# Graph attention and mixture-of-experts layer: row gathers without fills, slot sums by three strided reductions, partial step fourth

## The reference

```python
feat = einsum('ni,rhid->rnhd', layernorm(x), conv_weights)      # 8 types, 4 heads, 64 each
e = leaky_relu(el[type, src] + er[type, dst], 0.2)              # one score per edge and head
alpha = exp(e - segment_max(e, dst)) / segment_sum(exp(...), dst)
x = x + segment_sum(alpha * feat[type, src], dst) + h_bias
xf = layernorm(x)
cw = the two largest of softmax(xf @ gate_w + gate_b), else 0   # [3750, 8]
x = x + sum over e of cw[:, e] * (gelu(xf @ W1[e] + b1[e]) @ W2[e] + b2[e])
```

## Time and profile before

| | |
|---|---|
| median of 3 runs | 1844.96 us |
| profiled execution: its time, its span | 1841.54 us, 1839.5 us |
| busy: PE, DVE, ACT, POOL | 1291.8, 1294.8, 778.6, 1334.4 us |
| share of the span | 70%, 70%, 42%, 73% |
| mean granted TensorE clock | 0.838 of 2.4 GHz |
| phase 1, phase 2 | 258 us, 1581 us |

### The profile page before, as it was taken

How to read it: one execution, slowest core, us unless ns; L and a number is a source line. 1 busy time by engine, 2 the same in 40 slices (tenths; PEclk the granted TensorE clock), 3 DMA queues, 4 the chain that set the end, 5 groups by cost and what they waited for, 6 DMA issues and landing times.

```text
span 1839.5 us, 28715 instructions
## 1 busy us (share of the span) xinstructions
PE 1291.8 (70%) x6881; PEld 1040.7 (57%) x6881; DVE 1294.8 (70%) x2578; ACT 778.6 (42%) x2829; POOL 1334.4 (73%) x1702
## 2 busy tenths in 40 slices
PE   6999940037684777677767677777777685867787
PEld 2444420026574666666666566667666575756675
DVE  7660032668887888787878787878787878878881
ACT  3544410225354444444444444444444444544441
POOL 0727748688788788888888888888888888888600
PEclk9999975568797888888888888888879797888887
DMA  8758576333333333333333333333333333333300
GB/s 227 228 160 216 162 212 210 82 93 100 83 100 94 89 99 100 101 98 101 99 99 101 100 98 101 98 101 101 100 99 99 98 100 101 99 99 101 81 4 4
DMA packets 86819, 204.06 MB, mean 111 GB/s; under 512 B 32475, under 2 KB 44693, under 8 KB 82371
## 3 DMA queue, kind: packets, MB, share of 16 engines
q0 software_dynamic: 57552, 147.97, 29.8%
q10 hardware_dynamic: 9596, 33.95, 6.1%
q1 hardware_dynamic: 19485, 20.52, 4.0%
HBM read 162.22 MB, written 40.07 MB: 110 GB/s over the span
## 4 chain that ended last, share of the span: by engine, by line
POOL 41%; issue 18%; DVE 12%; PE 5%; DVEq 3%; POOLq 3%; ACT 2%; DMA 1%; ACTq 0%; SPq 0%
POOL rows L907 31%; POOL space_ring L940 7%; DVE fold_ps L1084 3%; PE y_ps L1511 2%; PE hid_ps L1497 2%; DVEq L67 2%; DVE rows L1080 1%; DVE xo L1236 1%; ACT rows L1400 1%; POOL out_dram L915 1%; POOL space_edge L940 1%; POOL xrows L907 1%; POOLq L920 1%; POOLq L964 1%; POOLq L979 1%
## 5 line engine op out<-in xcount | busy, mean ns | idle before, releaser
L907 POOL DMA_INDIRECT rows<-table,idx_st x982 | 943.5, 961 | 253.1 <-issue 243.8
L1511 PE MATMUL y_ps<-w,hT 128*128 128x256 f32 (+1 forms) x1920 | 508.3, 421 | 258.7 <-ACT hT L1389 258.7
L1511 PEld LDWEIGHTS y_ps<-w,hT 128*128 128x128 f32 (+1 forms) x1920 | 385.9, 208 | 345.8 <-ACT hT L1389 282.9
L1497 PE MATMUL hid_ps<-zT,w 128*128 128x128 f32 (+1 forms) x3840 | 497.3, 293 | 0.0
L1497 PEld LDWEIGHTS hid_ps<-zT,w 128*128 128x128 f32 x3840 | 485.9, 208 | 13.3 <-issue 10.8
L1400 ACT ACTIVATE rows<-rows,ex 128x65 f32<-128x65 f32 x1320 | 326.0, 346 | 114.0 <-DVE ex L1071 114.0
L1389 ACT ACTIVATE hT<-hid_ps,b1t 128x128 f32<-128x128 f32 (+1 forms) x960 | 269.6, 363 | 209.9 <-PE hid_ps L1497 208.5
L1084 DVE TENSOR_TENSOR fold_ps<-rows,fold_ps 128x780 f32<-128x780 f32 (+1 forms) x348 | 326.9, 939 | 34.1 <-issue 4.7
L598 PE MATMUL feat_ps<-wc,xnT 128*125 128x512 f32 x480 | 220.7, 604 | 0.5 <-ACT xnT L533 0.5
L1080 DVE TENSOR_TENSOR rows<-rows,fold_ps 128x2340 f32<-128x2340 f32 (+1 forms) x76 | 189.7, 2529 | 3.3 <-issue 3.3
L940 POOL MEMSET space_ring<- 128x400 uint8 x414 | 187.3, 452 | 0.1
(11 more groups left out here) (197 smaller groups left out, 1117.3 us busy)
## 6 DMA issues: line engine op xcount, KB each, us to landing
table<-stage ACTq DMA_DIRECT2D x30, 924.0 KB
rows<-table,idx_st POOLq DMA_INDIRECT x982, 2.8
w<-in_L_ffn_W_dram SPq DMA_DIRECT2D x16, 512.0 KB, 13.8
node_row<-ranked SPq DMA_DIRECT2D x30, 132.0 KB, 2.6
table<-stage ACTq DMA_DIRECT2D x30, 107.2 KB
x_all<-in_x_dram SPq DMA_DIRECT2D x2, 1120.0 KB
wc<-_L_gnn_conv_weights_dram ACTq DMA_DIRECT2D x2, 1024.0 KB, 8.0
attnb<-in_L_gnn_attn_l_dram SPq DMA_DIRECT2D x1, 1024.0 KB, 12.5
```

The source lines that it names most:

```text
L907: q.indirect_dma_start(buf[:, k, :], None, table, bass.IndirectOffsetOnAxis(idx[:, col + k:col + k + 1], 0)).then_inc(landed, 16)
L1497: last = t.matmul(hid_ps[e % 2][:, m * P:m * P + n], w1[:, e, k, m * P:(m + 1) * P], zT[:, k, 0:n], start=(k == 0), stop=(k == KD - 1))
L1511: last = t.matmul(y_ps[p % 2][0:n, (e % 2) * D:(e % 2 + 1) * D], hT[e % 2][:, k, 0:n], w2[:, e, k, :], start=(k == 0), stop=(k == KH - 1))
```

## The change

Three things. The fills and their semaphore go, so that POOL issues one gather after another. `weigh_all` sums slots 0 to 11, 12 to 20 and 21 to 31 with one `tensor_reduce` each, which reads the rows across the slots: neighbouring inputs of a sum are 264 floats apart. The first two write `part`, the third writes `acc`; two additions of 260 elements join them. In heavy windows slots 32 to 39 are added to slots 12 to 19 by one addition of 2080 elements. The three lanes and half of the PSUM tensor `fold_ps` are gone. Last, group 15 becomes window 1, group 16 window 29, 17 window 27 and so on down to group 28 in window 5, and the partial group 29 is window 3. Its 90 empty places get node numbers from 3750 on; every scatter is now of 128 rows with a bounds check that skips these, and the last window's expert work has 128 columns in place of 38.

```diff
-            sp.dma_start(ranked_v[LAST:P, W - 1, :], zeros[:]).then_inc(zero_out, 16)
+            sp.dma_start(ranked_v[LAST:P, 3, :], zeros[:]).then_inc(zero_out, 16)
...
-            g.memset(zeros[:], 0).then_inc(pool_const, 1)
+            g.memset(zeros[:, 0:D], 0).then_inc(pool_const, 1)
+            g.memset(zeros[:, D + 1:XW], 0).then_inc(pool_const, 1)
+            g.iota(zeros[:].bitcast(I32)[:, D:D + 1], pattern=[[1, 1]], base=N, channel_multiplier=1).then_inc(pool_const, 1)
...
-            go(v.tensor_scalar(tmpT[:], rank_f[:], -2.0, 2.0 * W - 3.0, ALU.mult, ALU.add))
+            go(v.tensor_scalar(tmpT[:], rank_f[:], -2.0, 2.0 * W + 1.0, ALU.mult, ALU.add))
...
-            go(v.tensor_scalar(tmpT[:], rank_f[:], 0.0, float(W), ALU.is_lt, ALU.mult))
+            go(v.tensor_scalar(tmpT[:], rank_f[:], float(W), 1.0 - W, ALU.is_ge, ALU.mult))
...
-            q.indirect_dma_start(out, bass.IndirectOffsetOnAxis(oid[par][0:n, :], 0), xo[par][0:n, :],
-                                 None).then_inc(out_done[par], 16)
+            q.indirect_dma_start(out, bass.IndirectOffsetOnAxis(oid[par][:], 0), xo[par][:], None,
+                                 bounds_check=N - 1, oob_is_err=False).then_inc(out_done[par], 16)
...
-            def spaced_gather(k):
-
+            def row(k):
                 gather(rows[par], row_landed[par][min(k // SLOTS, 2)], idx_st[par], (k,))
-                if k % 2:
-                    return q.memset(spacing(k // 2), 0)
-
-            def fills(n):
-                pool.wait_ge(spaced, n)
-                alone(pool, pool_passed)
...
             for k in range(SURE):
-                if k == 2 * EDGE and (not isinstance(w, int) or w >= 1):
-                    fills(w * 3)
-                if k == SLOTS and (not isinstance(w, int) or w >= 3):
+                if k == 2 * SLOTS and (not isinstance(w, int) or w >= 3):
                     scatter(w - 3, 1 - par)
...
-        def add(par, lo, n=LANES):
-
-            return v.tensor_tensor(lanes[:, 0:n], rows[par][:, lo:lo + n, 0:AGG], lanes[:, 0:n], ALU.add)
+        def summed(par, lo, hi, out):
+
+            return v.tensor_reduce(out, rows[par][:, lo:hi, 0:AGG].rearrange("p k c -> p c k"), AX_X, ALU.add)
 
         def weigh_all(w, par, st, between):
 
 
-            st.did(weighted(par, 0, LANES, lanes))
-            st.did(weighted(par, LANES, 12))
+            st.did(weighted(par, 0, 12))
             st.did(weighted(par, 12, ACT_LO))
             degree = dve.value_load(nb_row[0:1, bass.ds(w * 2 + 1, 1)], min_val=0, max_val=E)
             st.wait()
...
             with dve.If(degree > PAIRED * SLOTS):
                 weighted(par, PAIRED * SLOTS, NS)
                 dve.drain()
-                for lo, n in ((32, 3), (35, 3), (38, 2)):
-                    add(par, lo, n)
-                    dve.drain()
-            for lo in (3, 6):
-                st.did(add(par, lo))
-                st.wait()
+                v.tensor_tensor(rows[par][:, 12:12 + SLOTS, 0:AGG], rows[par][:, 12:12 + SLOTS, 0:AGG],
+                                rows[par][:, PAIRED * SLOTS:NS, 0:AGG], ALU.add)
+                dve.drain()
+            st.did(summed(par, 0, 12, part[:, 0, :]))
+            st.wait()
             dve.sem_inc(freed, 1)
-            for lo in (9, 12, 15):
-                st.did(add(par, lo))
-                st.wait()
+            st.did(summed(par, 12, ACT_LO, part[:, 1, :]))
+            st.wait()
             dve.sem_inc(freed, 1)
-            st.did(add(par, 18))
+            st.did(v.tensor_tensor(part[:, 0, :], part[:, 0, :], part[:, 1, :], ALU.add))
             between()
             st.wait()
             dve.wait_ge(act_weighed, w + 1)
-            st.did(add(par, 21))
-            st.wait()
-            dve.sem_inc(freed, 1)
-            for lo in (24, 27):
-                st.did(add(par, lo))
-                st.wait()
-            st.did(add(par, 30, 2))
-            st.wait()
-            dve.sem_inc(freed, 1)
-            st.did(v.tensor_copy(acc_f, lanes[:, 0]))
-            st.wait()
-            st.did(v.tensor_tensor(acc_f, acc_f, lanes[:, 1], ALU.add))
-            st.wait()
-            v.tensor_tensor(acc_f, acc_f, lanes[:, 2], ALU.add).then_inc(acc_ok, 1)
+            st.did(summed(par, ACT_LO, ACT_HI, acc_f))
+            st.wait()
+            dve.sem_inc(freed, 2)
+            v.tensor_tensor(acc_f, acc_f, part[:, 0, :], ALU.add).then_inc(acc_ok, 1)
...
-        experts(u, LAST)
+        experts(u)
```

More of the change, by code:

```diff
@@ L386, in _ @@
             v.memset(ones[:], 1.0).then_inc(ones_ok, 1)
-            dve.wait_ge(pool_const, 5)
+            dve.wait_ge(pool_const, 7)
             st.did(v.tensor_copy(bin_f[:], bin_i[:]))
@@ L651, in phase2 @@
     SURE = 20
-    LANES = 3
     ACT_LO, ACT_HI = 21, 32
@@ L679, in phase2 @@
     hot9 = sb("hot9", [P, NS, R1])
[L680 to L684, removed]
     er_hot = sb("er_hot", [P, NS, H, R1])
@@ L694, in phase2 @@
     acc_f = acc[:].rearrange("p h c -> p (h c)")
+    part = sb("part", [P, 2, AGG])
     r4 = sb("r4", [P, H])
@@ L732, in phase2 @@
     gate_ps, zt_ps = bank("gate_ps"), bank("zt_ps")
-    fold_ps = env["ctx"].enter_context(nc.psum_tensor("fold_ps", [P, 1024], F32))
-    lanes = fold_ps[:, 0:LANES * AGG].rearrange("p (k c) -> p k c", k=LANES)
-    at = LANES * AGG
+    fold_ps = bank("fold_ps")
+    at = 0
     ex_ps = fold_ps[:, at:at + H * NS].rearrange("p (h k) -> p h k", h=H)
@@ L909, in gather, with scatter @@
                                      ).then_inc(landed, 16)
-        def scatter(v, par, n=P):
+        def scatter(v, par):
             pool.wait_ge(out_ok, v + 1)
             alone(pool, pool_passed)
-            q.indirect_dma_start(out, bass.IndirectOffsetOnAxis(oid[par][0:n, :], 0), xo[par][0:n, :],
-                                 None).then_inc(out_done[par], 16)
+            q.indirect_dma_start(out, bass.IndirectOffsetOnAxis(oid[par][:], 0), xo[par][:], None,
+                                 bounds_check=N - 1, oob_is_err=False).then_inc(out_done[par], 16)
         def static_rows(w, par, half):
@@ L954, in static_rows @@
                     freed_by(k // SLOTS)
-                last = spaced_gather(k)
-                if k in (SURE // 2 - 1, SURE - 1):
-                    last.then_inc(spaced, 1)
+                row(k)
             if isinstance(w, int):
@@ L966, in more @@
                             freed_by(3)
-                        if k in (SURE, SURE + SURE // 2 - 2 * EDGE):
-                            fills(w * 3 + (1 if k == SURE else 2))
-                        spaced_gather(k)
+                        row(k)
                         more(k + 1)
             more(SURE)
-            q.memset(space_end[par][:], 0).then_inc(spaced, 1)
         def window(w, par, half):
@@ L1008, in _ @@
         scatter(W - 2, 0)
-        scatter(W - 1, 1, LAST)
+        scatter(W - 1, 1)
         for i in range(2):
@@ L1074, in exps, with weighted @@
             return st
-        def weighted(par, lo, hi, out=None):
+        def weighted(par, lo, hi):
             r = rows[par][:, lo:hi, 0:AGG].rearrange("p k (h c) -> p k h c", h=H)
-            o = r if out is None else out.rearrange("p k (h c) -> p k h c", h=H)
-            return v.tensor_tensor(o, r, bc(ex_ps[:, :, lo:hi].rearrange("p h k -> p k h"), 3, HC), ALU.mult)
-        def add(par, lo, n=LANES):
-            return v.tensor_tensor(lanes[:, 0:n], rows[par][:, lo:lo + n, 0:AGG], lanes[:, 0:n], ALU.add)
+            return v.tensor_tensor(r, r, bc(ex_ps[:, :, lo:hi].rearrange("p h k -> p k h"), 3, HC), ALU.mult)
+        def summed(par, lo, hi, out):
+            return v.tensor_reduce(out, rows[par][:, lo:hi, 0:AGG].rearrange("p k c -> p c k"), AX_X, ALU.add)
         def weigh_all(w, par, st, between):
-            st.did(weighted(par, 0, LANES, lanes))
-            st.did(weighted(par, LANES, 12))
+            st.did(weighted(par, 0, 12))
             st.did(weighted(par, 12, ACT_LO))
@@ L1322, in _ @@
         for p in range(PAIRS):
-            mix(u, 1, p, st, LAST)
+            mix(u, 1, p, st)
         finish(u, 1, st)
@@ L1457, in _ @@
         for e in range(NE):
-            gelu(u, e, LAST)
+            gelu(u, e)
             if e == 1:
```

11 lines of the change are left out of this document (2 added, 9 removed).

## The result

The changed kernel takes 1948.8 us (median of 4 runs, 1946.2 to 1950.3) against 1846.1 us (4 runs) for the kernel before on the same chip: ratio 1.055, interval 1.054 to 1.057. It is slower by 102.7 us. The forecast was 1957 us, 112 us slower.

A forecast was written before the change was run, and what follows sets the result against it. POOL and DVE were taken as two bounds 3 us apart in 95.6. Windows +153.3, waits for rows -32.9, waits for PE -11.4, start +1.6, tail +1.1 gave +111.7 on 1844.96: 1957 us, range 1925 to 1985.

The forecast's parts named there:

- What bounds the kernel: Window loop: POOL is full and DVE nearly so, two bounds 3 us apart in 95.6 us a pair.
- The fills: POOL's gathers: some 490 fills at 0.31 us, 150 us of POOL's time; the end gains at most 32.9 us.
- Light and heavy windows: DVE's sum over slots: light 24.6 us, 5.55 more; heavy 29.3 us, 5.0 more; strided element 1.89 ns.
- DVE's busy time: Sign in the profile after: DVE busy some 180 us longer, about 1475 us.
- The waits that go: DVE's waits: those for gathered rows give back 32.9 us, those for PE ahead of mixing 11.4 us.
- Start: Up to window 1: 20 fills saved, 6 us sooner, then group 15's gathers 7.6 us later; +1.6 us.
- Tail: Last window with 128 columns for 38: first expert pair +0.8 us, GELU +0.3 us; +1.1 us.
- The sum: Whole kernel: windows +153.3, rows -32.9, PE -11.4, start +1.6, tail +1.1, together +111.7 us; 1957 us.
- B: Rival on DVE's reductions: the stride costs nothing, 1.04 ns an element, 9.1 us a window; 1763 us, chance 0.13.
- C: Rival on POOL: gathers in long runs without a fill cost more, 1.19 us + 0.30; 1987 us, chance 0.06.
- D: Rival on DVE's reductions: the stride costs two full cycles, 2.08 ns; +46 us, 2003 us; chance 0.13 with E.
- E: Rival on PE: it waits longer for `z`, its clock falls further; +39 us, 1996 us; chance 0.13 with D.

The follow-up runs named there:

- e1_nofills: The kernel before without its fills and nothing else: 1796.4 us, ratio 0.975.
- e2_reduces: The kernel before, fills and order kept, with the strided reductions in place of the additions: 1951.6 us, ratio 1.059.
- e3_order: The kernel before with only the new window order, the bounds check and the last window's 128 columns: 1830.8 us, ratio 0.994.
- e5_strides: The changed kernel with reductions and additions at many distances appended: 1.04 ns an element up to two floats, 1.67 to 1.83 from four on.
- e7_halving: The kernel before without fills, its lanes replaced by contiguous additions folding the slots in place in SBUF: 1849.0 us, ratio 1.004.
- e9_tail128: The kernel before, old order, with the last window's experts on 128 columns in place of 38: 1837.0 us in a single execution.
- e11_nofills_tail128: The kernel before without fills and with the last window's experts on 128 columns: 1792.9 us, ratio 0.972.
- e4_contig: The changed kernel with its reductions reading as many elements from neighbouring places, output meaningless: 1772.7 us, ratio 0.962.

## Why the prediction was right, step by step

**What bounds the kernel.** Right: POOL and DVE are two bounds some 3 us apart in a pair of windows. e1_nofills moves POOL's alone and gains 46 us, e2_reduces moves DVE's alone and loses 109.5.

**The fills.** Right, and somewhat too small. Waits for rows from window 1 on vanish in e1_nofills, and most of its 46 us are those 35.7 and a start that is 8.7 us sooner (407.16 to 398.44). A gather costs 0.96 us with fills and without.

**Light and heavy windows.** Right: 24.59 and 29.30 us against 24.6 and 29.3. It is partly two errors that cancel. The price of an element was 1.81 ns and not 1.89, which makes the three reductions 0.63 us cheaper in a window (15.55 against 16.2). But the addition into `part` is followed by 0.48 us of idleness before mixing that I left out. Over windows 1 to 29 my rows give 14 x 5.50 + 15 x 5.04 = 152.6 us, and DVE is busy 154.2 us longer there.

**DVE's busy time.** The sign to look for, some 180 us more, was not what the prediction's own terms give: 14 x 5.55 + 16 x 5.04 is 158 us for windows 0 to 29. DVE is busy 157.8 us longer (1452.6 against 1294.8).

**The waits that go.** Nearly right. The windows' part is 104.6 us, so all that is not in those 152.6 gave 48.0 us back, where 44.3 were forecast. Waits for rows give 35.7, those for PE ahead of mixing 11.4; `zt_ps` at L1187 takes 4.4 (7.0 less 2.6), `r` at L1125 gives 3.0 (21.5 less 18.5). Some 2 us weren't followed.

**Start.** The term was too small: +6.1 us against +1.6. Of the difference of 4.5 us, 3.0 are no cost of the change: phase 2's first gather starts 3.0 us later (261.22 against 258.21), but in e3_order and e5_strides, which have all of the new work of phase 1, it starts at 257.70 and 258.59; such 3 us lie between executions. One gather takes 2.50 us in place of 0.95, and that is a cost of the change. It starts 0.7 us into the new addition of 2080 elements, both of whose operands are in SBUF, and ends 0.8 us behind it, as the held gathers of e7_halving do:

```profile
325.78 2.33 DVE L1069 TENSOR_TENSOR rows<-rows 128x2080 f32<-128x2080 f32 x1
```

```profile
326.44 2.50 POOL L902 DMA_INDIRECT rows<-table,idx_st  x1 [0.30 <-issue]
```

What is left agrees with the 7.6 - 6 us of the forecast.

**Tail.** The sign was wrong: -4.2 us against +1.1. I took the price of 128 columns from a first product that stood behind 5 us of idleness and 38 columns as the cheaper case. e9_tail128 and e11_nofills_tail128 show the opposite, -4.9 and -3.8 us.

**The sum.** Its nearness is in part luck: the start came out 4.5 us above its term, the windows 4.4 and the tail 5.3 us below theirs. The further 3.8 us between the spans' +106.5 and the medians' +102.7 lie between executions.

**The rivals.** B, no price for the stride, is what e4_contig makes of the kernel, 1773 us against the 1763 worked out for it; its cause, a price that depends on the distance in such a way that 1056 bytes are free, is refuted by the reductions of the changed kernel and by e5_strides. That the forecast's price was taken from neighbours 120 bytes apart did little harm, since the price doesn't rise between 16 and 2560 bytes; e5_strides has 1.83 ns at 120 bytes and 1.78 at 1056. The tier table by which `tensor_reduce` has one rate (the Trainium skill, VectorE: DVE Perf Modes, The perf-mode tier table) holds up to two floats; from four on the measurement decides, 1.8 ns. C, dearer gathers in long runs: 0.95 to 0.98 us in the mean in every kernel but e7_halving, which has a cause of its own; refuted. D, two full cycles: 1.81 ns and not 2.08. E, PE and its clock: the granted clock did fall, from 0.85 to 0.81 in windows 1 to 29, but the wait for PE at L1187 is never over 0.8 us, so it costs little.

## What to carry to other kernels

When two engines are almost equally full, cost the change on both: relief for the one (46 us alone here, 38 of them in windows 1 to 29) is worth next to nothing there (2 us, order included) once the other has been made the bound. Before a tree of contiguous additions is replaced by a reduction across a layout, count read elements times the strided price; here 8320 at 1.81 ns lost to a tree that read contiguous rows, though the tree had more instructions. Find the price in any instruction of the same kind that already runs with a stride, however small: one 1920-element reduction decided this forecast.

## What the runs showed that was not expected

- **An addition with both operands in SBUF holds up GpSimd's gathers.** Gathers of 957 ns became 1120 in the mean and 3.00 us under a 2.87-us addition, and went back to 956 ns when one operand came from PSUM: 61 us of the kernel. The Trainium skill (SBUF — State Buffer, Who interferes with whom) says that a DVE instruction with two inputs in SBUF contends with GpSimd instructions that read SBUF, and infers that the making of DMA descriptors is not held by a `tensor_tensor`. The first agrees with these runs; by the second e7_halving's gathers would have kept their 957 ns, and there the measurement decides. One such addition is in the changed kernel as well, in the heavy windows; in window 0 it holds a gather for 2.50 us.
- **Fewer columns were slower.** At full clock a pair of experts' products takes 7.4 us with 38 columns as with 128; but with 38 the granted clock falls in the first pairs of the window (0.62 and 0.76 in the first pair's products, against 1.00), and the last window takes 4 to 5 us more.
- **A reorder can pay by moving the bound's work into the start**: in e3_order windows 1 to 29 took 18.4 us less although its start was 12.6 us later, some 6 us in all beside the 5 of the last window's columns. Added to a kernel in which POOL was no longer the bound, the same edit lost 13 us.
- **The price of a stride is a step between two and four floats**, with no rise from there to 640 (1.67 to 1.83 ns an element).
